# Turn of a layer pipeline: a later split, output norms behind the sigmoid, a projection in front of G

## The reference

```python
qkv = x @ Wqkv + bqkv;  q, k, v = split(qkv)          # attention without a softmax
q -= mean(q); k -= mean(k)
q2 = q*q / (sum(q*q) + eps);  q2 = q2 / l2norm over the columns
k2 = k*k / (sum(k*k) + eps);  k2 = k2 / l2norm over the rows
kv = k2.T @ v;  t2 = q2 @ kv / sqrt(N)
x1 = layernorm(x + (v + t2) @ Wln + bln)
sel = sigmoid(x1 @ expert_sel.T)                       # 16 experts, all of them used
out = sum over e of relu(x1 @ keys[e]) @ values[e] * sel[:, e]
result = layernorm(x1 + out)
```

## Time and profile before

| | |
|---|---|
| median of 3 runs | 1004.89 us (1000.58 to 1005.08) |
| the profiled execution | 1000.15 us, its span 998.2 us |
| PE busy | 982.9 us (98%) |
| PEld busy | 941.8 us (94%) |
| DVE busy | 808.5 us (81%) |
| ACT busy | 527.8 us (53%) |
| POOL busy | 57.5 us (6%) |
| granted TensorE clock, mean | 0.999 |

### The profile page before, as it was taken

How to read it: one execution, slowest core, us unless ns; L and a number is a source line. 1 busy time by engine, 2 the same in 40 slices (tenths; PEclk the granted TensorE clock), 3 DMA queues, 4 the chain that set the end, 5 groups by cost and what they waited for, 6 DMA issues and landing times.

```text
span 998.2 us, 20891 instructions
## 1 busy us (share of the span) xinstructions
PE 982.9 (98%) x7718; PEld 941.8 (94%) x7718; DVE 808.5 (81%) x1874; ACT 527.8 (53%) x1150; POOL 57.5 (6%) x75
## 2 busy tenths in 40 slices
PE   8999999999999999999999999999999999999997
PEld 7898999999999999999999999999999999999997
DVE  6889887988778887888878898788987888878546
ACT  6557635475445653556435664455644566354323
POOL 0000101001010100101001010010100101010100
PEclk9999999999999999999999999999999999999999
DMA  5163234432343223441342613325133342333232
GB/s 188 36 208 97 77 106 132 147 95 85 114 142 138 77 99 118 135 159 65 104 139 88 190 64 108 118 96 182 60 112 114 104 165 76 107 105 103 89 95 68
DMA packets 75912, 112.45 MB, mean 113 GB/s; under 512 B 7202, under 2 KB 38178, under 8 KB 75812
## 3 DMA queue, kind: packets, MB, share of 16 engines
q1 hardware_dynamic: 75812, 111.13, 34.4%
HBM read 87.51 MB, written 23.46 MB: 111 GB/s over the span
## 4 chain that ended last, share of the span: by engine, by line
PE 76%; DVE 10%; DMA 5%; issue 4%; ACT 3%; SPq 1%; POOL 0%; DVEq 0%; ACTq 0%; POOLq 0%
PE down_bank L1406 27%; PE up_bank L1406 27%; PE ring_bank L1406 9%; PE qk_bank L1406 6%; PE g_bank L1406 4%; DMA sel_all<-sel_out 3%; DVE gated_l L1144 2%; DVE gated L1162 1%; DMA parked_x<-w_room 1%; SPq L478 1%; DVE x1T_l L1008 1%; ACT L666 1%; PE g_bank L1459 1%; DVE z_stats L1106 1%; DVE qk L1162 1%
## 5 line engine op out<-in xcount | busy, mean ns | idle before, releaser
L1406 PE MATMUL down_bank<-vals_h,gated_h 128*128 128x256 f32 x1024 | 285.9, 279 | 2.8 <-DVE gated_l L1144 2.8
L1406 PE MATMUL down_bank<-vals_l,gated_h 128*128 128x256 f32 x1024 | 283.6, 277 | 0.0
L1406 PE MATMUL down_bank<-vals_h,gated_l 128*128 128x256 f32 x1024 | 283.6, 277 | 0.0
L1406 PE MATMUL up_bank<-x1T_h,keys_h 128*128 128x256 f32 (+1 forms) x928 | 268.1, 289 | 0.3 <-DVE gated L1162 0.3
L1406 PE MATMUL up_bank<-x1T_l,keys_h 128*128 128x256 f32 (+1 forms) x928 | 268.2, 289 | 0.0
L1406 PE MATMUL up_bank<-x1T_h,keys_l 128*128 128x256 f32 (+1 forms) x928 | 268.2, 289 | 0.0
L598 ACT ACTIVATE gated_h<-gated 128x512 fp32r<-128x512 f32 x176 | 111.3, 632 | 199.7 <-DVE gated L1162 199.7
L1406 PEld LDWEIGHTS down_bank<-vals_h,gated_h 128*128 128x128 f32 x1024 | 192.2, 188 | 9.3 <-DVE gated_l L1144 5.1
L1406 PEld LDWEIGHTS down_bank<-vals_l,gated_h 128*128 128x128 f32 x1024 | 192.9, 188 | 4.1
L1406 PEld LDWEIGHTS down_bank<-vals_h,gated_l 128*128 128x128 f32 x1024 | 192.3, 188 | 0.0
L1162 DVE SCALAR_TENSOR_TENSOR gated<-up_bank,sel_all 128x512 f32<-128x512 f32 x176 | 121.4, 690 | 76.1 <-PE up_bank L1406 56.1
(11 more groups left out here) (278 smaller groups left out, 1782.5 us busy)
## 6 DMA issues: line engine op xcount, KB each, us to landing
sel_all<-sel_out SPq DMA_DIRECT2D x192, 256.0 KB, 3.7
x_raw<-in_x SPq DMA_DIRECT2D x15, 512.0 KB, 5.8
out<-z SPq DMA_DIRECT2D x30, 256.0 KB, 2.5
xT_raw<-in_xT SPq DMA_DIRECT2D x14, 512.0 KB, 5.4
parked_q<-w_room SPq DMA_DIRECT2D x14, 512.0 KB, 2.6
q<-parked_q SPq DMA_DIRECT2D x56, 128.0 KB, 3.0
parked_x<-w_room SPq DMA_DIRECT2D x14, 512.0 KB, 3.0
w_room<-parked_x SPq DMA_DIRECT2D x56, 128.0 KB, 3.0
```

Of the source, the lines that this page charges most:

```text
L1406: last = mm(dst, lhs, rhs, start=start and i == 0, stop=stop and i == n - 1, **kw)
```

## The change

Three edits, and what they bring along:

- XR of the first group (the split of the turned x1) moves from step 27 to step 28. So ACT copies it behind `gated_h` of step 28, and DVE subtracts behind gate(29).
- `norm_steps` moves the output norms of both pairs into step 31, behind the sigmoid, and SP's two stores with them. ACT runs a one-column sigmoid at the end of step 30 (`table_ahead`), so that the sigmoid's table is loaded there. The sigmoid of the logits moves behind `gated_h` of step 31, and `gated_l` of step 31 is no longer late.
- In step 12 the projection QK of tile 4 stands in front of G's share GG of tile 2.

```diff
-        12: [("GG", 2), ("QK", 4), ("LG", 1), ("QS", 1)], 13: ...
+        12: [("QK", 4), ("GG", 2), ("LG", 1), ("QS", 1)], 13: ...
-        25: [("QR", 1), ("XS", 3)], 27: [("XR", 0)], 29: [("ZN", 0)], 30: [("LG", 0), ("ZN", 1)],
+        25: [("QR", 1), ("XS", 3)], 28: [("XR", 0)], 29: [("ZN", 0)], 30: [("LG", 0), ("ZN", 1)],
+        def norm_steps(s):
+            return {STEPS - 2: (), STEPS - 1: (STEPS - 3, STEPS - 2)}.get(s, (s - 1,))
         def low_is_late(it, s):
-            return gate_room(s) is not gate_room((s + 1) % STEPS) and (it, s) != (B - 1, STEPS - 1)
+            return gate_room(s) is not gate_room((s + 1) % STEPS) and s != STEPS - 1
 # SP, step
-                    elif kind == "ZN":
-                        store_pair(it, off, a)
...
+                for n in norm_steps(s + 1) if s < STEPS - 2 else norm_steps(s):
+                    for kind, a, off in planned(it, n, ("ZN",)):
+                        store_pair(it, off, a)
 # ACT, end of late, and step
-                if not last_iteration(it):
-                    output_norms(it, s - 1)
+                if s == STEPS - 2 and planned(it, s, ("LG",)):
+                    nc.scalar.activation(table_ahead[:, 1:2], eps_ln[:], ACT.Sigmoid)
+                for n in norm_steps(s):
+                    if not last_iteration(it):
+                        output_norms(it, n)
-                early(it, s, ("KS", "LG"))
+                early(it, s, ("KS",) if s == STEPS - 1 else ("KS", "LG"))
...
+                if s == STEPS - 1:
+                    early(it, s, ("LG",))
```

More of the change, by code:

```diff
@@ L745, in output_norms @@
                     for i in range(1 if last_iteration(it) else 2):
-                        nc.scalar.activation(z_room(it)[:, a, i], z_room(it)[:, a, i], ACT.Identity, bias=z_shift[:, a, i:i + 1],
+                        nc.scalar.activation(z_room(it)[:, a, i], z_room(it)[:, a, i], ACT.Identity,
+                                             bias=z_shift[:, a, i:i + 1],
                                              scale=z_rstd[:, a, i:i + 1]).then_inc(out_made, 1)
             def step(it, s):
-                early(it, s, ("KS", "LG"))
+                early(it, s, ("KS",) if s == STEPS - 1 else ("KS", "LG"))
                 if step_exists(it, s):
```

## The result

The changed kernel takes 1015.62 us (median of 6, 1011.77 to 1016.94), the kernel before 1004.96 on the same chip: ratio 1.0108, interval 1.0083 to 1.0133. It is slower by 1.1%, about 11 us. I had forecast 1006.2 with a range up to 1011.0, so it fell outside, on the side of rival B.

A forecast was written before the change was run, and what follows sets the result against it. PE's matmuls and stops were taken to bound the kernel; -4.0 (step 1) - 2.6 (step 12) + 10.3 (step 30) - 0.2 (last batch) = +3.5 us, from 1002.7 to 1006.2, range 1001.0 to 1011.0.

The forecast's parts named there:

- rival B: At gate(29), the xT load delays the row, so step 30's stop is larger: +7.3 us, 1010.0; chance 22%.
- Step 1: At the turn, down(31) no longer waits for gated_l in any of seven turns: minus 4.0 us.
- Rival C: At the turn, gated_l of step 31 still ends late, so the 4.0 stay: +7.5 us, 1010.2; chance 5%.
- Step 12: The projection in front of G starts on time and covers the wait for k_l: minus 2.6 us.
- Step 30: LG stops PE because x1T_l stands behind gate(29), which waits for its DMA row: plus 10.3 us.

The follow-up runs named there:

- e2: Only the edit of the turn, made on the kernel before: ratio 0.9962 to the kernel before.
- e3: Only the projection put in front of G in step 12, on the kernel before: ratio 1.0024 to the kernel before.
- e4: The changed kernel with XR back in step 27, turn and projection edits kept: ratio 0.9994 to the kernel before.
- e13: The changed kernel with G's share in front of the projection in step 12 again: ratio 1.0111 to the kernel before.
- e7: The changed kernel with DVE's bias addition of step 11 put earlier, in front of k_total: ratio 1.0129 to the kernel before.
- e5: The changed kernel, but DVE makes x1T_l in front of gate(29), XR staying in step 28: ratio 0.9985 to the kernel before.
- e9: The changed kernel with x1T_l made in front of gate(29) and G's share in front of the projection again: ratio 0.9968 to the kernel before.
- e6: The changed kernel, but SP issues the row of step 29 one step earlier, before the turn's DMAs: ratio 0.9991 to the kernel before.
- e12: The kernel before, unchanged, executed a second time: profiled span 1002.49 us.
- e8_best: The changed kernel with XR back in step 27, step 29's row issued earlier and step 11's bias addition earlier: ratio 0.9968 to the kernel before.
- e1: Only the split of the turned x1 moved to step 28, on the kernel before: ratio 1.0097 to the kernel before.
- e11: The changed kernel, unaltered, run again: ratio 1.0108 to the kernel before, profiled span 1006.13 us.
- e15: The changed kernel, unaltered, executed a third time: profiled span 1008.43 us.

## Why the prediction was wrong

**Step 1, minus 4.0: right.** No turn stops in any profile that has the edit, and e2 measures minus 3.8 us. Rival C is out.

**Step 12, minus 2.6, bounds minus 2.9 and minus 1.9: this step failed.** The stop went as I said (2.88 to 1.59; 0.87 and 0.57 in the other two executions), the saving did not come: plus 2.4 us alone (e3), plus 3.2 beside the turn (e4 against e2), minus 0.3 beside the late split (changed against e13), the last two uncertain by 2 to 4 us. I had written that above minus 1.9 nothing would be lost, and had called the stretches between the three places solid. Two things were wrong with that. First, I never asked where the next release lies: DVE's `x_l` in step 20 had nothing to spare before, so a PE that is 0.4 earlier waits there instead (rows above), and the stretch from step 12 to step 20 is not shorter in any pair of kernels. Second, a stop leaves something behind. The stop at G had put PE on the fast pace each time, and in its place came a release just late enough to put it on the slow one in 18 of 42 cases. I had seen the 0.17 between the addition and PE and called it on time. How the loss of 2.4 to 3.2 us divides between slow pace and other late releases is not shown; e13 and e7, which take the flips away, gained nothing measurable beside the late split.

**Step 30, plus 10.3: the mechanism and the stops were right, as time it was too small.** Gate(29) at its row's landing, `x1T_l` 1.21 behind it, LG 0.14 behind that: all as worked out (I had 0.15, and 2 x 0.61 for the split). The first two distances at LG are too long by 11.4, 12.2 and 12.8 us in the three executions, where I had 10.9 + 0.5. What the sum had at nothing is the clock. Iteration 4 lost 1.3 us more in step 30 since the clock fell behind LG's stop (last section), so that the step has 12.7. As time, the late split is worth 12.3 us with the projection in front (e5), 14.3 with G in front (e13 against e9), 11.4 by e4 and 14.9 by e2 against e13. The new stops at LG are 10.3 to 11.7 of it, so up to some 4 us are something else. Falls of the clock are part of that, 1 to 2 us in the mean (last section); the rest stays open.

**Rival B** named the right side, not the reason: it wanted a mean lateness of 1.8 us. The row landed 1.00 to 2.09 us behind the start of down(27), 1.57 in the mean, where I had 1.56 and where B decides from 1.8. The row's landing (4.4 in iteration 2) is what it was the earlier trace rows.
By the fit of the Trainium skill ("DMA: Bandwidth & Descriptors", section "Anatomy of one DMA"), made on GpSimd's path, this transfer would take an estimated 2.6 us. Even in e6, where the row goes ahead of the turn's reads, it takes 3.1 (iteration 2), so the trace does not agree there either, though that is nearer.

**The sum** can't be put right term by term, since the terms depend on the order in which the edits are made. From the kernel before by e2 and e4 to the changed one it is -3.8 + 3.2 + 11.4 = +10.8 us (turn, step 12, step 30), by e2 and e13 it is -3.8 + 14.9 - 0.3 = +10.8; I had -4.0 - 2.6 + 10.3 - 0.2 = +3.5. Of the 7.3 us between, step 12 has 5.8 by the first way and 2.3 by the second, step 30 the rest but for 0.4. By both ways the saving in step 12 did not come.

**The range** was too narrow for the same reason: every term was a stop at one of three places, and I never put a price on the pace, though the kernel before shows both paces in its own trace. Between executions of the same kernel the slow pace alone moved a span by 4 to 5 us (e12 against the two others).

**Open.** How much of the slow pace belongs to the change (8.3 to 16.3 us against 5.0 to 10.1, three executions each), and why the medians of e13 and e7 don't show what their distances do. For e13 the clock is part of the answer: its profiled execution has one fall (mean granted clock 0.997), while three of the five others have means of 0.994 and 0.995. It is not all of it: the one at 0.999 took 1010.63 us, 3.9 more than the profiled one.

## What to carry to other kernels

Before a stop of the bounding engine is removed, look for its next release behind it, and at how much that has to spare: here the 0.4 us saved in step 12 were waited for again in step 20. The end of the releasing instruction against the start of the one that it releases shows it, even where no wait is listed.

A stop is not only its own length either: ask in what state it leaves the engine, and compare the distance of its instructions in the stretch behind it before and after. A release 0.17 us ahead of PE was not in time here, one 0.56 ahead was.

Before an operation that the bound waits for is put behind a gate with a DMA in front, look at the latest landing of that DMA, not at the wait seen so far; other work can cover it.

The edit of the turn alone (e2_turn_only, 0.9962) does as well as anything measured here: e8_best and e9_g_first_split (both 0.9968), which add the projection or the split, each with its cure, can't be told apart from it. All three beat both kernels.

## What the runs showed of the hardware

**Two paces of TensorE.** Matmuls of 256 columns start 113.3 or 117.8 ns apart, with the same operands and with the granted clock at 1.00, for hundreds in a row (1066 of them from 463 to 620 us in the changed kernel). What turns it in step 12: a release late by about 0.05 us, in 18 of 42 cases. What brings it back: the stop at G, in 8 of 8 (table and rows above). LG's stop does both: in the three profiles of the changed kernel it brought PE back five times and turned it slow five times.

**The clock after a stop.** In iteration 4 of the changed kernel PE stood still for 2.09 us at LG. The stretches before, behind and after that (us, busy per engine, granted clock, DMA share, GB/s):

```profile
650.00:655.90 5.90, 3.98 (x36) 3.81 (x34) 2.69 (x5) 1.78 (x3) 0.00 (x0) 1.00 0.74 240
655.90:659.30 3.40, 3.40 (x12) 3.02 (x13) 3.37 (x13) 1.81 (x5) 0.00 (x0) 0.50 0.02 5
659.30:664.00 4.70, 4.70 (x37) 4.43 (x36) 2.82 (x7) 3.40 (x6) 0.60 (x1) 1.00 0.00 0
```

The granted clock is 0.50 (1.2 GHz) for 3.4 us and then 1.00 (2.4 GHz) again, which costs about half of the 3.4, an estimate from the two levels. It is seen once in the changed kernel, three times in e1 (286.2, 654.8, 777.7) and once in e13 (530.5), each time within 1.6 us of the end of a stop of 2.0 to 2.5 us at LG; but not in e11, nor in e15, whose iteration 1 lost 2.4 us there, nor in e7, whose iteration 4 lost 2.6. What decides between them I did not find.

The falls belong to the late split. Of the 27 executions of kernels with it (changed with e11 and e15, e1, e7, e13), 17 have a mean granted clock of 0.993 to 0.997. In all other executions on record but the one of e4 named above, some 190, it is 0.998 or 0.999. The means over the executions, 0.9973 for the six of the changed kernel in the section on the result and 0.9962 for e13 against 0.9985, make 1.2 and 2.3 us of a span (estimates: the share lost times the span).
